# Post-layernorm attention and int8 FFN on eight cores: rounding on VectorE, the final layernorm in two full ScalarE passes, and one semaphore per chunk of the transposed input

## The reference, cut to what matters

```
h = layernorm(x + attention(x) @ WO.T)            # 16 heads, causal softmax
n = h * rsqrt(mean(h*h) + 1e-6)                   # rms norm
s = 127 / max(|n|)   (per row)
q = clip(round(n * s), -128, 127)
f = (q / s) @ (w_int8 * weight_scale).T + bias
out = layernorm(h + f)
```

## Time and profile before

| | before |
|---|---|
| median of 3 runs | 1795.81 us (1794.53 to 1796.21) |
| the profiled execution's own time | 1797.55 us |
| its span on the slowest core (core 2) | 1795.9 us |
| spans of the 8 cores | 1772.3 to 1795.9 us |
| busy share of the span: PE, ACT, DVE, POOL | 71%, 50%, 31%, 17% |
| stage `ph45` of batch 0 on core 2 | about 624 to 891 us |
| PE stands still, end of batch 0 to start of batch 1 | 47.9 us |

### The profile page before, as it was taken

How to read it: one execution, slowest core, us unless ns; L and a number is a source line. 1 busy time by engine, 2 the same in 40 slices (tenths; PEclk the granted TensorE clock), 3 DMA queues, 4 the chain that set the end, 5 groups by cost and what they waited for, 6 DMA issues and landing times.

```text
span 1795.9 us, 25317 instructions; the slowest of 8 cores (1772.3 to 1795.9 us)
## 1 busy us (share of the span) xinstructions
PE 1271.7 (71%) x8710; PEld 594.9 (33%) x8710; DVE 551.4 (31%) x1615; ACT 901.0 (50%) x1252; POOL 305.5 (17%) x603
## 2 busy tenths in 40 slices
PE   1999778777777766666409987877777777575564
PEld 0444333334343422222104443334434443222221
DVE  1001322211111266667400012322111113666664
ACT  0332126687788634444403322177878784444444
POOL 1000222322212101111300002222221211111111
PEclk9999776577778778777759997755777777867786
DMA  9333003000000011111590330030000000112111
GB/s 158 53 48 47 1 1 48 1 1 1 1 1 1 1 47 71 67 63 59 101 156 1 47 47 1 1 48 1 1 1 1 2 1 12 48 59 71 66 53 47
DMA packets 23005, 64.54 MB, mean 36 GB/s; under 512 B 1379, under 2 KB 2403, under 8 KB 22884
## 3 DMA queue, kind: packets, MB, share of 16 engines
q0 software_dynamic: 18272, 46.14, 13.5%
q1 hardware_dynamic: 4612, 16.78, 3.1%
HBM read 75.50 MB, written 16.78 MB: 51 GB/s over the span
## 4 chain that ended last, share of the span: by engine, by line
PE 32%; ACT 23%; DVE 13%; issue 9%; POOL 9%; DMA 5%; DVEq 4%; ACTq 4%; POOLq 0%
ACT PT L489 17%; PE psall L280 13%; POOL PT L514 9%; PE psall L325 8%; PE psall L388 5%; PE psall L406 4%; ACTq L787 4%; DMA xT<-xt 2%; DVEq L683 2%; DMA wslotA<-wqt 2%; DVE dump L688 2%; ACT x1b L788 2%; DVE dumpb L691 2%; PE psall L432 2%; ACT x1b L785 2%
## 5 line engine op out<-in xcount | busy, mean ns | idle before, releaser
L489 ACT ACTIVATE PT<-psall,ebias 128x1024 bf16<-128x1024 f32 x448 | 468.3, 1116 | 310.0 <-PE psall L388 310.0
L388 PE MATMUL psall<-QT,KT 64*128 64x512 bf16 (+3 forms) x1280 | 282.0, 451 | 126.1 <-ACT PT L489 111.4
L406 PE MATMUL psall<-Vx,PT 128*128 128x65 bf16 x4352 | 302.6, 216 | 85.4 <-POOL PT L514 83.8
L514 POOL TENSOR_TENSOR PT<-PT,mask 128x128 bf16<-128x128 bf16 x512 | 200.6, 425 | 704.7 <-ACT PT L489 704.4
L406 PEld LDWEIGHTS psall<-Vx,PT 128*128 128x128 bf16 x4352 | 210.2, 110 | 247.6 <-issue 236.7
L849 PE MATMUL psall<-wslotB,qT 128*128 128x512 bf16 x512 | 181.4, 532 | 42.4 <-ACT qT L833 42.4
L551 DVE RECIPROCAL rinv<-psall 128x4 f32<-128x4 f32 x64 | 11.7, 183 | 637.2 <-PE psall L406 637.2
L280 PE MATMUL psall<-xT,wslotA 128*128 128x512 bf16 x512 | 115.6, 390 | 83.3 <-DMA xT<-xt 47.9
L338 DVE CAST Vx<-psall 128x512 bf16<-128x512 f32 x64 | 44.3, 692 | 356.9 <-PE psall L325 356.9
L325 PE MATMUL psall<-wslotA,xT 128*128 128x512 bf16 x512 | 148.0, 460 | 0.0
L388 PEld LDWEIGHTS psall<-QT,KT 64*128 64x128 bf16 x1280 | 68.1, 97 | 227.7 <-issue 206.0
(11 more groups left out here) (99 smaller groups left out, 903.1 us busy)
## 6 DMA issues: line engine op xcount, KB each, us to landing
xstg<-x SPq DMA_DIRECT2D x32, 512.0 KB, 3.6
y<-outst POOLq DMA_DIRECT2D x32, 512.0 KB, 3.1
xT<-xt POOLq DMA_DIRECT2D x4, 1024.0 KB, 22.2
wslotA<-wqt POOLq DMA_DIRECT2D x2, 2048.0 KB, 30.2
wslotB<-wkt POOLq DMA_DIRECT2D x2, 2048.0 KB, 49.5
wslotA<-wvt POOLq DMA_DIRECT2D x2, 2048.0 KB, 16.9
wslotB<-w8t POOLq DMA_DIRECT2D x2, 2048.0 KB, 16.3
wslotA<-wot POOLq DMA_DIRECT2D x2, 2048.0 KB, 17.6
```

Of the source, the lines that this page charges most:

```text
L388: last = eng.matmul(out, lhsT, rhs, start=True, stop=True, skip_group_check=True)
L406: last = eng.matmul(out, lhsT, rhs, start=(i_glob < 2), stop=(i_glob >= n_total - 2), skip_group_check=True)
L489: eng.activation(PT[:, pt * 1024:(pt + 1) * 1024], psall[:, p * 1024:(p + 1) * 1024], AF.Exp, bias=ebias[:, :], scale=0.125).then_inc(sem_ ...
L514: last = eng.tensor_tensor(blk, blk, mask01[:, :], ALU.mult)
```

## The change

The edit has three parts.

1. The rounding moves from ACT to DVE. `SBr` and `VC2` are gone; `VC(t)` on DVE now scales (L780 of the changed kernel), adds RC and -RC in one instruction with two immediate operands, in place (L785), and clips (L788), with a drain between them.
2. `SD(t)` no longer makes the row bias `-mean * rs` by a 128x1 activation (L902 before). ACT instead subtracts the mean from the whole 128x1024 tile z in place (L892), drains, and then scales it with a zero bias (L895). No drain stands between the root (L890) and the first pass.
3. sem_gx is replaced for xT by four semaphores, one for each chunk of two of the eight 128-row blocks. Only the first group of 8 matmuls waits for them, before its matmuls 0, 2, 4 and 6.

```diff
-                eng.dma_start(dst, src).then_inc(sem_gx, 16)
+                eng.dma_start(dst, src).then_inc(sem_xc[c], 16)
...
-                    W("t", "gx", xt_done)
...
+                        first_g = (proj == 0 and dt == 0 and sch == 0)
...
                             for kt in range(8):
+                                if first_g and kt % 2 == 0:
+                                    eng.wait_ge(sem_xc[kt // 2],
+                                                xt_done[kt // 2])
...
                     eng.tensor_scalar(x1b2h(t), z[:, :],
                                       sc[:, c0 + 7:c0 + 8],
                                       sc[:, c0 + 12:c0 + 13],
-                                      ALU.mult,
-                                      ALU.add).then_inc(sem_v, 1)
-                emit("v", f7)
-                qvA[t] = bump("v")
-
-            def SBr(t):
-                W("s", "v", qvA[t])
-                def f7b(eng, t=t):
-                    eng.activation(x1b2h(t), x1b2h(t), AF.Identity,
-                                   bias=rcol[:, :], scale=1.0)
-                    eng.drain()
-                    eng.activation(x1b2h(t), x1b2h(t), AF.Identity,
-                                   bias=nrcol[:, :],
-                                   scale=1.0).then_inc(sem_s, 1)
-                emit("s", f7b)
-                rdone[t] = bump("s")
-
-            def VC2(t):
-                W("v", "s", rdone[t])
-                def f7c(eng, t=t):
+                                      ALU.mult, ALU.add)
+                    eng.drain()
+                    eng.tensor_scalar(x1b2h(t), x1b2h(t), RC, -RC,
+                                      ALU.add, ALU.add)
+                    eng.drain()
                     eng.tensor_scalar(qih(t), x1b2h(t), 127.0,
                                       -128.0, ALU.min,
                                       ALU.max).then_inc(sem_v, 1)
...
                     eng.activation(sc[:, c2 + 2:c2 + 3],
                                    sc[:, c2 + 1:c2 + 2], AF.Sqrt)
-                    eng.drain()
-                    eng.activation(sc[:, c2 + 4:c2 + 5],
-                                   sc[:, c2 + 3:c2 + 4], AF.Identity,
-                                   scale=sc[:, c2 + 2:c2 + 3])
+                    eng.activation(z[:, :], z[:, :], AF.Identity,
+                                   bias=sc[:, c2 + 3:c2 + 4], scale=1.0)
                     eng.drain()
                     eng.activation(
                         outst2[:, (t % 2) * 1024:(t % 2) * 1024 + 1024],
-                        z[:, :], AF.Identity, bias=sc[:, c2 + 4:c2 + 5],
+                        z[:, :], AF.Identity, bias=zcol[:, :],
                         scale=sc[:, c2 + 2:c2 + 3]).then_inc(sem_s, 1)
```

More of the change, by code:

```diff
@@ L126, in build_nc @@
         sem_xd2 = e(nc.semaphore("sem_xd2"))
+        sem_xc = [e(nc.semaphore(f"sem_xc{c}")) for c in range(4)]
         block = e(nc.Block())
@@ L131, in build_nc @@
         ctr = {k: 0 for k in ("t", "v", "s", "g", "d", "gd", "o",
-                              "gx", "gb", "o2", "xd", "xd2")}
+                              "gx", "gb", "o2", "xd", "xd2",
+                              "xc0", "xc1", "xc2", "xc3")}
         SEM = {"t": sem_t, "v": sem_v, "s": sem_s, "g": sem_m,
                "d": sem_d, "gd": sem_g, "o": sem_o, "gx": sem_gx,
-               "gb": sem_gb, "o2": sem_o2, "xd": sem_xd, "xd2": sem_xd2}
+               "gb": sem_gb, "o2": sem_o2, "xd": sem_xd, "xd2": sem_xd2,
+               "xc0": sem_xc[0], "xc1": sem_xc[1], "xc2": sem_xc[2],
+               "xc3": sem_xc[3]}
         def emit(engine, fn):
@@ L227, in f @@
                                  (2048, 2), (1, 2048))
-                        eng.dma_start(dst, src).then_inc(sem_gx, 16)
+                        eng.dma_start(dst, src).then_inc(sem_xc[c], 16)
                     emit("g", f)
-                    bump("gx", 16)
-                xt_done = ctr["gx"]
+                    bump(f"xc{c}", 16)
+                xt_done = {c: ctr[f"xc{c}"] for c in range(4)}
             def wload(w_handle, slot, wait_t):
@@ L271, in ph1, with f @@
                             W("t", "s", s_evac.get(half - 4))
-                        def f(eng, dt=dt, sch=sch, half=half, slot=slot):
+                        first_g = (proj == 0 and dt == 0 and sch == 0)
+                        def f(eng, dt=dt, sch=sch, half=half, slot=slot,
+                              first_g=first_g):
                             out = pslot(half)
                             for kt in range(8):
+                                if first_g and kt % 2 == 0:
+                                    eng.wait_ge(sem_xc[kt // 2],
+                                                xt_done[kt // 2])
                                 lhsT = wslot[slot][
@@ L607, in ph45 @@
             appd2 = {}
-            qvA = {}
-            rdone = {}
             NP = 16
@@ L799, in f7c @@
                                       ALU.max).then_inc(sem_v, 1)
-                emit("v", f7c)
+                emit("v", f7)
                 qv[t] = bump("v")
@@ L935, in ph45 @@
                 VC(t)
-                SBr(t)
-                VC2(t)
                 G_x1pb(t)
@@ L954, in ph45 @@
                     VC(i + 2)
-                    SBr(i + 2)
-                    VC2(i + 2)
                     G_x1pb(i + 2)
@@ L1014, in fb @@
                                      (16384, 128), (2048, 2), (1, 256))
-                            eng.dma_start(dst, src).then_inc(sem_gx, 16)
+                            eng.dma_start(dst, src).then_inc(sem_xc[c], 16)
                         emit("g", fb)
-                        bump("gx", 16)
-                    nxt["xt"] = ctr["gx"]
+                        bump(f"xc{c}", 16)
+                    nxt["xt"] = {c: ctr[f"xc{c}"] for c in range(4)}
             cb = preload_cb if b + 1 < BPC else None
```

## The result

The changed kernel takes 1716.66 us (median of 9 runs) where the kernel before, measured beside it, takes 1794.99 us (median of 10). The median is inside the predicted range and 15.7 us above the predicted 1701.

What follows compares the result with a forecast made beforehand. The tile loop was taken as bound by DVE's own work plus the detour over ACT. Batch 0 44.9, restart 2.5 and batch 1 47.3 give 94.7 us off 1797.55: 1702.9, by the runs' median 1701; range 1690 to 1726.

Steps and rivals of the forecast that it cites:

- the turn that the forecast of 1701 stands on: Tile loop, VD to VD: 12.94 us instead of 16.22, a gain of 3.28 in each turn.
- the prediction's own sign: New profile, tile loop: forecast wrong if the turn exceeds 13.5 us; L686's row then names PE, store or load.
- rival A: Tile loop: PE becomes the bound, FFN and projection both slow, turn 14.6 us; 1741, or 1721 for half; chance 0.16.
- The wait that goes: Tile loop, DVE: clip no longer waits for ACT, starts at 5.30 us instead of 8.99; rounding pass priced at 0.81.
- The pass on ACT: Tile loop, SD: new in-place pass takes 1.15 us, SD ends at 6.21; VA waits 0.41, so ACT sets the turn.
- Does PE fit: Tile loop: PE's projection ends 5.77 us into the next turn, needed at 6.32; it fits, so nothing is charged.
- B: Tile loop: SD is not the new bound, DVE sets the turn at 12.53 us; 1691; chance 0.07.
- C: Tile loop: late stores hold SD and stop the loop, turn 17.5 us; 1811, slower; chance 0.03.
- D: Tile loop: another wait, for x or the FFN, replaces the removed one; at most 16 us gained, 1780; chance 0.04.
- The prologues: Tiles 0 and 1 ahead of each loop: DVE's wait for ACT shrinks, 1.56 us saved twice, 3.1 a batch.
- the way to WQ: End of batch 0, VD(12) to the issue of WQ: 9.53 us instead of 11.91, a gain of 2.4.
- After VD(12) of batch 1: End of batch 1, last two tiles: 5.5 us gained, 0.7 given back by the longer SD, net 4.8.

Runs made afterwards that it cites:

- e5: Kernel before with only the rounding moved to DVE, old final layernorm and single xT semaphore kept: 1714.25 us, ratio 0.9559.
- e1: Changed kernel plus ten fill matmuls, results unread, ahead of each output projection: 1700.4 us, ratio 0.9494.
- after: Profile of the changed kernel itself, all three parts in: profiled execution 1712.42 us, median of the runs 1716.66 us.
- e2: Changed kernel with the final layernorm on ACT put back as before (128x1 bias, one full pass): 1713.5 us, ratio 0.9553.
- e9: Changed kernel plus four fill matmuls, instead of ten, ahead of each output projection: 1714.76 us, ratio 0.9554.
- e3: Changed kernel plus ten fill matmuls ahead of each projection, with the old final layernorm on ACT: 1692.3 us, ratio 0.9437.
- e6: Changed kernel with one semaphore for xT again instead of four: 1719.2 us, ratio 0.9612.
- e4: Kernel before with only the two-pass final layernorm on ACT added, rounding left on ACT: 1814.7 us, ratio 1.0114.

## Why the prediction was right in part, and where it failed

The time lies in the range, but the turn that the forecast of 1701 stands on did not come. By the prediction's own sign it was wrong there: the turn is above 13.5 us and the row of L686 names PE. The range held 1717 because it had been stretched to half of rival A, which came in by another road than the one it was priced by. That the number is covered is in part luck.

- **The wait that goes (part 1).** Right. The clip no longer waits for ACT, and e5 shows that this part alone has the whole gain. The rounding pass takes 0.69 us, the lower bound of its price, not the 0.81 taken. The Trainium skill, VectorE: DVE Perf Modes, the perf-mode tier table, gave an estimate of 0.7 for it; the trace agrees.
- **The pass on ACT (part 2).** Sized right, 1.13 us against 1.15, and SD ends at 6.17 against 6.21. That it sets the turn was right only for turns in which PE is fast: e1 shows the predicted wait of 0.4 us in most of its turns, after does not.
- **Does PE fit.** This is the step that failed, as it stood: "At the longest of these rows, 6.54, they end at 15.09 ...; the output projection, 3.62, ends at 5.77. ... It fits by half a microsecond, so I charge nothing". Each row was taken for a property of its matmuls. They were a pair: the projection had 3.62 because an FFN of 6.54 ran right up to it. With a shorter turn PE's earlier pause shrank from 4.53 us to almost nothing, the FFN ran at 1.00 and ended early, and the pause moved to the place between FFN and projection, where VD(i) must first read the buffer. The projection then cost 5.30 instead of 3.62: VA came at 6.98 instead of 6.32, 0.66 us in each of 24 turns, 16 us. That is what the two loops fell short by (16.3). Between the two profiled spans the whole shortfall is only 94.7 - 85.5 = 9.2 us, because the other terms gave some 3 us more than they were charged at and the stretches without an edited line some 4.5. That the projection's low clock is what closes the circle, and that filling the pause mends it, is shown by e1, e2 and e9. That the FFN became fast because its own pause went is my reading; no run changes that pause alone, and in e1 some FFNs are slow behind a pause of 1.8 us or less.
- **Rival A** named the resource, a projection at the low clock, and half of its price gave 1721. Its form was wrong: it took both matmul groups as slow and counted PE's busy time, 14.6 us. In fact the FFN became fast, and PE is not busy throughout; it is one link in a circle with DVE. The argument against A, "the projection follows the FFN directly, as now", is the sentence that the trace refutes: 2.94 us lie between them. The Trainium skill, TensorE: Matmul & The Clock Gate, Part 1, that idle time brings the throttle back, was cited for the forecast; the trace of after agrees with the rule (0.54 behind the pause of 2.94 us), and it spoke against the forecast, since the denser loop had an idle place that I had not looked for.
- **Rivals B, C and D** did not occur in the loops. The stores landed after 3.0 us in the median; B's turn of 12.53 is what e3 reaches (12.39) by taking the second pass out.
- **Outside the loops.** The prologues gave 3.5 and 3.6 (3.1 predicted; the cheaper rounding accounts for 0.1 a tile), the way to WQ 2.3 (2.4). After VD(12) of batch 1 it was 6.5 instead of 4.8, because the last FFN ran at the high clock there: 3.61 instead of 5.30.

```profile
1679.53 1.28 DVE L857 SCALAR_TENSOR_TENSOR z<-psall,w2a,x1b 128x1024 f32<-128x1024 f32 x1
...
1695.27 3.61 PE L840 MATMUL psall<-wslotB,qT 128*128 128x512 bf16 x16 [1.31 <-ACT qT L824]
```

These are VD(12) and the FFN of tile 15 in after, core 5, and answer to the earlier trace rows. Part 3 was worth 2.4 us by the landings (e6), 2.5 predicted, and stays unproved by the times. The 4.2 us between the first chunk's landing and PE's start, from which the 2.5 was worked out, were read off a semaphore on which all the loads count; with a semaphore each, the chunks land some 2 us apart, first to last, as they were issued.

## What to carry to other kernels

When a loop gets shorter, work out again where each engine pauses, and take no matmul time from a row without what ran ahead of it: a matmul group that was fast because a slow one led up to it can be slow when that one gets faster. A circle of waits is priced link by link (here VD, projection, VA), not by comparing each engine's busy time with the turn. If PE is a link in the circle and pauses ahead of it, work whose result nobody reads can pay for itself; try it together with the control in a kernel where PE is not in the circle, and look at every turn afterwards, since the low clock can settle on another matmul group.

## What the runs showed that I had not expected

- Work added to PE made the kernel faster: ten matmuls, 2.32 us in each turn, took 13 us off the time (1713.5 in e2 to 1700.4 in e1, same chip, SD's old form being worth nothing there), and none off the kernel before (ratio 1.0020).
- Four fill matmuls had no part of the effect of ten: with 2.08 us of pause left the projection took 5.30 us, as with 2.94; with 0.17 and 0.72 us left it took 3.61.
- In after and e9 the granted clock reads 1.00 throughout the pause and is low only once the matmuls start again (0.54 in after, 0.51 in e9). The clock in these pauses alone shows nothing. In the longer pause of the kernel before (722.60 to 727.10, ahead of the transposes) it reads 0.78: there it fell within the pause.
- The two-pass SD costs 20 us in the kernel before (e4), nothing in the loops of the changed one (e2), and 8 us once PE is fast (e3 against e1): one edit with three prices, by what binds the turn.
